# Cross attention on one Trainium2 core: a unit's softmax shift goes from TensorE to VectorE, and GpSimd pre-adds halves of exponentials

## The chip, the cores and the metric

One core of one Trainium2 chip runs the whole kernel; seven cores are idle. The metric is the device time of one execution in microseconds (us), from the chip's own clock. TensorE is PE in the profile, VectorE is DVE, ScalarE is ACT, GpSimd is POOL, SyncE is SP.

## The reference

The model is a small "audio tower": token selection, a retention layer, a top-1 mixture of experts, a cross attention, and a top-2 mixture of experts. The change is in the cross attention:

```
q = (text @ Wq.T + bq)          # 8 batches x 512 rows, 2 heads of 64
k = (video @ Wk.T + bk)         # 128 videos x 64 frames
v = (video @ Wv.T + bv)
logits = einsum('avhd,bthd->abhvt', k, q) / sqrt(64)
weights = softmax(logits, axis=3)        # over the 64 frames of one video
attn = einsum('avhd,abhvt->abhtd', v, weights).mean(over the 128 videos)
out = attn @ Wo.T + bo
```

Every one of the 4096 rows is scored against all 8192 frames in both heads, with a softmax of its own for each of the 128 videos: a maximum over 64 frames, a shift by it, an exponential, a sum over 64, a division.

## The kernel before, in words

The attention stage runs through **8 batches** of queries (`B`), in each through 16 chunks of 512 keys (`NKC`), and takes each chunk for the 512 rows of the batch in two **steps** of 256 rows. That is 32 steps to a batch (a "run" in the code) and 256 in all. A step works on four **units** (`UNITS`): unit j is one head (j % 2) and one tile of 128 rows (j // 2), its data 128 rows x 512 keys, that is 8 videos of 64 frames. Units 0 and 1 are pair 0, units 2 and 3 are pair 1. The logits of unit j live in bank j of `psL`, its weights in one of eight slots of `weights` (two parities of four).

What a unit goes through: two matmuls give the logits (L1754, L1755; queries split into a high and a low part); VectorE takes the negated maxima of a pair in one reduction of 128x1024 (L1840); the logits are shifted by them; ScalarE takes the exponential; VectorE sums the exponentials of a pair (L1856) and inverts the sums of all four units (L1862); GpSimd multiplies each unit's weights by them (L1945); TensorE transposes the weights, four blocks a unit (L1774); ScalarE copies the result out (L1908); TensorE multiplies by the values (L1788, "mix"), three steps after the logits.

Who does the shift is set by the table `SHIFTED_BY`: ScalarE for unit 0 (as the bias of eight small exponentials, L1901), TensorE for units 1 and 3 (one more matmul of the identity by the maxima into `psL`, L1764, then one exponential out of `psL`, L1893), VectorE for unit 2 (a tensor-tensor add out of `psL` into `weights`, L1850, then an exponential in place, L1896).

The order on each engine is written out by hand in its `step`. VectorE's step n before is: maximum of pair 0, `total(n - 1, ..., 1)`, `invert(n - 1)`, maximum of pair 1, the shift of unit 2, `total(n, ..., 0)`. TensorE's is: logits of pair 0, the shift of unit 3 of step n-1, transposes of pair 0 of step n-2, the mix of step n-3, the shift of unit 1, logits of pair 1, transposes of pair 1 of step n-2. GpSimd's is the four multiplications of step n-1, as soon as `invert(n - 1)` has run.

`steps_of` writes the first 8 steps of a run out flat (`FIRST`), where every semaphore count is a constant, and puts the other 24 in a hardware loop of 6 turns of 4 steps, where counts are computed in registers. In flat steps 1 and 3 the queries of the next batch are projected (L1746 on TensorE, L1886 on ScalarE, `low`, L1834, on VectorE).

An instruction that reads what its own engine has just written waits on a semaphore for it: the shift of unit 2 waits on `maxima_ready`, which the maximum just ahead of it raises, and then on `turned_ready`, since its slot of `weights` must have been transposed two steps before:

```
def subtract(n, parity, pair, reused):
    ...
        dve.wait_ge(maxima_ready, 2 * n + (pair + 1))
        if reused:
            dve.wait_ge(turned_ready, 4 * n + (j + 1 - 8))
        dve.tensor_tensor(...)
```

Of the kernel before, what the change touches and what calls it, by code (L numbers as in the profile page):

```python
# [20 lines left out]
ALU = mybir.AluOpType  # L21
# [1534 lines left out]
def cross_attention(nc, a, K):  # L1556
# [16 lines left out]
    with ExitStack() as ctx:  # L1573
# [10 lines left out]

        UNITS = 4
        STEPS, FIRST, LAG = 2 * NKC, 8, 3
        SHIFTED_BY = ("ScalarE", "TensorE", "VectorE", "TensorE")
        shifted_on = {who: [j for j in range(UNITS) if SHIFTED_BY[j] == who] for who in set(SHIFTED_BY)}
        keys_in = [sem(f"keys_in{s}") for s in range(2)]
        values_in = [sem(f"values_in{s}") for s in range(2)]  # L1590
# [58 lines left out]
        with ExitStack() as inner:  # L1649
# [15 lines left out]
            logits_ready, maxima_ready, exped = sem("logits_ready"), sem("maxima_ready"), sem("exped")  # L1665
            shifted, subtracted = sem("shifted"), sem("subtracted")
            summed, scales_ready, normalised = sem("summed"), sem("scales_ready"), sem("normalised")
            turned_ready, turned_copied = sem("turned_ready"), sem("turned_copied")
            chunks_mixed, run_copied = sem("chunks_mixed"), sem("run_copied")

# [36 lines left out]
            def exists(n):  # L1707

                return not isinstance(n, int) or 0 <= n < B * STEPS
# [4 lines left out]
            with nc.Block() as block:  # L1714
# [114 lines left out]
                @block.vector  # L1829
                def _(dve):  # L1830
                    def low(p, h, count):

                        dve.wait_ge(q_highs, count)
                        dve.scalar_tensor_tensor(q_low[p][h][:], psQ[:], K.bq2[:, h:h + 1], q_high[p][h][:].bitcast(F32),  # L1834
                                                 ALU.add, ALU.subtract).then_inc(q_lows, 1)

                    def maximum(n, pair):
                        dve.wait_ge(logits_ready, 4 * n + (2 * pair + 2))
                        both = slice(2 * pair, 2 * pair + 2)
                        dve.tensor_reduce(maxima[:, both, :].rearrange("p j v -> p (j v)"),  # L1840
                                          psL[:, both, :].rearrange("p j (v f) -> p (j v) f", f=FR), X, ALU.max, negate=True).then_inc(maxima_ready, 1)

                    def subtract(n, parity, pair, reused):
                        for j in (2 * pair, 2 * pair + 1):
                            if SHIFTED_BY[j] == "VectorE":
# [4 lines that stand above are left out]
                                dve.tensor_tensor(videos(weights[:, 4 * parity + j, :]), videos(psL[:, j, :]),  # L1850
                                                  maxima[:, j, :, None].bitcast(F32).to_broadcast([P, VC, FR]), ALU.add).then_inc(subtracted, 1)

                    def total(n, parity, pair):
                        both = slice(4 * parity + 2 * pair, 4 * parity + 2 * pair + 2)
                        dve.wait_ge(exped, 4 * n + (2 * pair + 6))
                        dve.tensor_reduce(sums[:, both, :].rearrange("p j v -> p (j v)"),  # L1856
                                          weights[:, both, :].rearrange("p j (v f) -> p (j v) f", f=FR), X, ALU.add).then_inc(summed, 1)

                    def invert(n, parity):
                        chunk = slice(4 * parity, 4 * parity + 4)  # L1860
                        dve.wait_ge(summed, 2 * n + 2)
                        dve.reciprocal(scales[:, chunk, :], sums[:, chunk, :]).then_inc(scales_ready, 1)  # L1862

                    def step(i, p, s, k, q4):
                        n, parity = index(i, p, s), k % 2
                        if exists(n):
                            maximum(n, 0)
                        if exists(n - 1):
                            total(n - 1, 1 - parity, 1)
                            invert(n - 1, 1 - parity)  # L1870
                        if exists(n):
                            maximum(n, 1)
                            subtract(n, parity, 1, exists(n - 2))
                            total(n, parity, 0)
                            if isinstance(s, int) and s in (1, 3):
                                low(1 - p, s // 2, (i * 2 + p) * 2 + (s // 2 + 3))

                    low(0, 0, 1)
                    low(0, 1, 2)
                    steps_of(dve, step)  # L1880
# [56 lines left out]

                @block.gpsimd
                def _(pool):
                    def normalise(n, parity, pair):  # L1940
                        for j in (2 * pair, 2 * pair + 1):
                            s = 4 * parity + j
# [4 lines left out]
                    def step(i, p, s, k, q4):  # L1947
                        n = index(i, p, s)
                        if exists(n - 1):
                            normalise(n - 1, 1 - k % 2, 0)  # L1950
                            normalise(n - 1, 1 - k % 2, 1)

                    steps_of(pool, step)
# [69 lines left out]
```

## Time and profile before

| | us |
|---|---|
| Time, median of 3 runs (2453.16 to 2456.1) | 2454.87 |
| Time of the profiled execution | 2457.68 |
| Span of the profiled execution | 2455.9 |
| Attention stage in it, about | 560 to 2140 |
| One step of the loop | 6.107 |
| One run of 32 steps | 197.14 |

The attention stage is two thirds of the time. Its steps repeat to within a hundredth of a microsecond, so that whatever a change does to one loop step it does 192 times (8 runs of 24), and to a flat step 64 times. In a timeline each row has the start of an instruction and its duration; two rows of one engine can overlap a little, so the cost of an instruction in a row of others is the distance from its start to the next start (called its pitch here), and not its duration.

### The profile page before, as it was taken

What the parts mean: (1) busy time and instruction counts of PE and PEld (TensorE: products, weight loads), DVE (VectorE), ACT (ScalarE), POOL (GpSimd) and SP (SyncE); (2) the same over time, 40 slices, a digit from 0 to 9 for tenths busy, and PEclk for the clock granted to TensorE, in tenths of its full rate; (3) what the DMA queues carried; (4) which work ended last, traced back from release to release, by engine and by line L of the source; (5) the groups of instructions that cost most, each with busy time, mean ns of one, the idle gap of its engine ahead of it and who ended that gap; (6) DMA issues with size and microseconds to landing.
All of it is one profiled execution on the core that took longest, in us unless ns stands there. A gap on an engine that the chain in (4) does not pass through costs nothing. (4 is left out here: it accounts for less than half of the span.)

```text
span 2455.9 us, 49808 instructions
## 1 busy us (share of the span) xinstructions
PE 2150.6 (88%) x14597; PEld 1692.2 (69%) x14597; DVE 1985.9 (81%) x3132; ACT 1689.1 (69%) x4826; POOL 1446.6 (59%) x1416
## 2 busy tenths in 40 slices
PE   4566876838999999999999999999999999967883
PEld 3345766825777777777777777777777777757883
DVE  6977764147999999999999999999999999866664
ACT  1154212516888888888888888888888888803662
POOL 2643433754666666666666666666666666623773
PEclk9675666968999999999999999999999999967997
DMA  7421023622222222222222222222222222143655
GB/s 242 142 69 44 28 60 94 168 60 61 65 64 65 65 64 64 65 64 64 65 64 64 65 64 64 65 64 64 65 65 64 64 65 64 43 96 101 156 154 154
DMA packets 157683, 197.68 MB, mean 80 GB/s; under 512 B 33200, under 2 KB 99888, under 8 KB 155504
## 3 DMA queue, kind: packets, MB, share of 16 engines
q1 hardware_dynamic: 139280, 174.80, 26.5%
q0 software_dynamic: 8064, 16.60, 2.5%
q10 hardware_dynamic: 10208, 4.66, 0.7%
q8 instruction: 67, 1.10, 0.2%
q14 instruction: 64, 0.52, 0.1%
HBM read 77.58 MB, written 17.74 MB: 39 GB/s over the span
## 5 line engine op out<-in xcount | busy, mean ns | idle before, releaser
L1945 POOL TENSOR_TENSOR attend_weights<-attend_weights,attend_scales 128x512 f32<-128x512 f32 x1024 | 1036.3, 1043 | 560.6 <-DVE attend_scales L1862 560.6
L1840 DVE TENSOR_REDUCE attend_maxima<-attend_psL 128x16 fp32r<-128x1024 f32 x512 | 624.5, 1220 | 89.5 <-PE attend_psL L1755 89.5
L1856 DVE TENSOR_REDUCE attend_sums<-attend_weights 128x16 f32<-128x1024 f32 x512 | 619.0, 1209 | 0.1
L1908 ACT ACTIVATE attend_turned<-attend_psT 128x512 f32<-128x512 f32 x1024 | 554.4, 596 | 9.0 <-PE attend_psT L1774 5.9
L1774 PE MATMUL attend_psT<-consts,attend_weights 128*128 128x128 f32 x4096 | 530.8, 272 | 0.8 <-POOL attend_weights L1945 0.8
L1774 PEld LDWEIGHTS attend_psT<-consts,attend_weights 128*128 128x128 f32 x4096 | 477.5, 140 | 66.1 <-POOL attend_weights L1945 1.3
L1788 PE MATMUL attend_psA<-attend_turned,attend_value_ring 128*64 128x256 f32 x4096 | 498.5, 385 | 0.8 <-ACT attend_turned L1908 0.8
L1901 ACT ACTIVATE attend_weights<-attend_psL,attend_maxima 128x64 f32<-128x64 f32 x2048 | 446.6, 329 | 53.1 <-DVE attend_maxima L1840 53.1
L1754 PE MATMUL attend_psL<-attend_key_ring,attend_q_high 128*128 128x512 f32 x1024 | 430.6, 420 | 1.6 <-ACT attend_q_high L1886 1.6
L1755 PE MATMUL attend_psL<-attend_key_ring,attend_q_low 128*128 128x512 f32 x1024 | 404.1, 395 | 0.0
L1788 PEld LDWEIGHTS attend_psA<-attend_turned,attend_value_ring 128*64 128x64 f32 x4096 | 271.5, 136 | 154.4 <-issue 43.7
L1893 ACT ACTIVATE attend_weights<-attend_psL 128x512 f32<-128x512 f32 x512 | 313.8, 613 | 0.0
L1896 ACT ACTIVATE attend_weights<-attend_weights 128x512 f32<-128x512 f32 x256 | 162.1, 633 | 128.6 <-DVE attend_weights L1850 128.5
L1764 PE MATMUL attend_psL<-attend_maxima,cross_ident_r 128*128 128x512 f32 x512 | 221.1, 432 | 6.1 <-DVE attend_maxima L1840 6.0
L1755 PEld LDWEIGHTS attend_psL<-attend_key_ring,attend_q_low 128*128 128x128 f32 x1024 | 194.6, 190 | 33.6 <-issue 3.8
L1754 PEld LDWEIGHTS attend_psL<-attend_key_ring,attend_q_high 128*128 128x128 f32 x1024 | 194.2, 190 | 30.3 <-issue 4.0
L1850 DVE TENSOR_TENSOR attend_weights<-attend_psL,attend_maxima 128x512 f32<-128x512 f32 x256 | 177.1, 692 | 25.8
L1764 PEld LDWEIGHTS attend_psL<-attend_maxima,cross_ident_r 128*128 128x128 f32 x512 | 95.9, 187 | 116.5 <-DVE attend_maxima L1840 99.6
L1448 ACT ACTIVATE moe2mix_hidT<-moe2mix_psH,moe_b 128x128 f32<-128x128 f32 x284 | 81.0, 368 | 57.6 <-PE moe2mix_psH L1401 57.4
L1363 POOL DMA_INDIRECT moe2mix_rows<-normed,moe_source x71 | 68.7, 968 | 79.0 <-POOLq L1134 50.9
L1862 DVE RECIPROCAL attend_scales<-attend_sums 128x32 f32<-128x32 f32 x256 | 90.4, 353 | 8.9
L1368 POOL DMA_INDIRECT result<-moe2mix_result,moe_target x71 | 70.8, 998 | 24.9 <-issue 16.8
(316 smaller groups left out, 2368.8 us busy)
## 6 DMA issues: line engine op xcount, KB each, us to landing
attend_key_ring<-keys SPq DMA_DIRECT2D x512, 128.0 KB, 2.2
attend_value_ring<-values SPq DMA_DIRECT2D x128, 256.0 KB, 2.5
moe2mix_w_tile<-in_L_ffn_w_dram SPq DMA_DIRECT2D x71, 256.0 KB
select_xbuf<-in_x_dram SPq DMA_DIRECT2D x16, 1024.0 KB, 5.4
moe1mix_w_tile<-in_L_ffn_W_dram SPq DMA_DIRECT2D x39, 256.0 KB, 3.1
select_emb<-L_attn_video_embeds_dram ACTq DMA_DIRECT2D x16, 256.0 KB, 4.3
values_gates<-project_vg SPq DMA_DIRECT2D x8, 512.0 KB, 2.6
retain_vg<-values_gates SPq DMA_DIRECT2D x8, 512.0 KB
```

Of the source, the lines that this page charges most:

```text
L1754: pe.matmul(psL[:, j, :], q_high[p][h][:, tile], key_ring[:, k // 2, h, :], start=True, stop=False, skip_group_check=True)
L1755: pe.matmul(psL[:, j, :], q_low[p][h][:, tile], key_ring[:, k // 2, h, :], start=False, stop=(SHIFTED_BY[j] != "TensorE"), skip_group_chec ...
L1764: pe.matmul(videos(psL[:, j, :]), ident_r[:], maxima[:, j, :, None].to_broadcast([P, VC, FR]), start=False, stop=True, skip_group_check=Tr ...
L1774: mm = pe.matmul(psT[:, j % 2, k * P:(k + 1) * P], weights[:, 4 * parity + j, k * P:(k + 1) * P], ident, is_transpose=True, start=(k == 0) ...
L1788: mm = pe.matmul(psA[head_rows(h), r * 2 * P:(r + 1) * 2 * P], value_ring[:, slot, h, t, :], turned[:, parity, t, h].rearrange("p t l -> p ...
L1840: dve.tensor_reduce(maxima[:, both, :].rearrange("p j v -> p (j v)"), psL[:, both, :].rearrange("p j (v f) -> p (j v) f", f=FR), X, ALU.ma ...
L1850: dve.tensor_tensor(videos(weights[:, 4 * parity + j, :]), videos(psL[:, j, :]), maxima[:, j, :, None].bitcast(F32).to_broadcast([P, VC, F ...
L1856: dve.tensor_reduce(sums[:, both, :].rearrange("p j v -> p (j v)"), weights[:, both, :].rearrange("p j (v f) -> p (j v) f", f=FR), X, ALU. ...
L1893: act.activation(into, psL[:, j, :], ACT.Exp).then_inc(exped, 1)
L1901: ins = act.activation(into[:, video], psL[:, j, video], ACT.Exp, bias=maxima[:, j, v:v + 1].bitcast(F32))
L1908: act.activation(turned[:, parity, :, h, t, :], psT[:, j % 2, :].rearrange("p (k q) -> p k q", k=SUB), ACT.Copy).then_inc(turned_copied, 1)
L1945: pool.tensor_tensor(w, w, scales[:, s, :, None].to_broadcast([P, VC, FR]), ALU.mult).then_inc(normalised, 1)
```

## The change

The second entry of `SHIFTED_BY` becomes VectorE, so that VectorE shifts units 1 and 2 and TensorE unit 3 alone. GpSimd gets a new instruction a step (`halve`): it adds the first 32 of every 64 exponentials of units 0 and 1 to the other 32, into a tile `halves` of 128x512, between its multiplications of units 0, 1 and of units 2, 3 of the step before. VectorE's sum of pair 0 then reads `halves` (512 elements) and not `weights` (1024), and stands one step later in the order: `total(n - 1, ..., 0)` beside `total(n - 1, ..., 1)`. The shift of unit 1 stands right behind the maximum of pair 0.

```diff
-        SHIFTED_BY = ("ScalarE", "TensorE", "VectorE", "TensorE")
+        SHIFTED_BY = ("ScalarE", "VectorE", "VectorE", "TensorE")
...
+            halves = sba("halves", [P, 2 * VC, FR // 2])
+            halved = sem("halved")
...
                     def total(n, parity, pair):
                         both = slice(4 * parity + 2 * pair, 4 * parity + 2 * pair + 2)
-                        dve.wait_ge(exped, 4 * n + (2 * pair + 6))
-                        dve.tensor_reduce(sums[:, both, :].rearrange("p j v -> p (j v)"),
-                                          weights[:, both, :].rearrange("p j (v f) -> p (j v) f", f=FR), X, ALU.add).then_inc(summed, 1)
+                        own = sums[:, both, :].rearrange("p j v -> p (j v)")
+                        if pair == 0:
+                            dve.wait_ge(halved, n + 1)
+                            dve.tensor_reduce(own, halves[:], X, ALU.add).then_inc(summed, 1)
+                        else:
+                            dve.wait_ge(exped, 4 * n + (2 * pair + 6))
+                            dve.tensor_reduce(own, weights[:, both, :].rearrange("p j (v f) -> p (j v) f", f=FR), X, ALU.add).then_inc(summed, 1)
...
                         if exists(n):
                             maximum(n, 0)
+                            subtract(n, parity, 0, exists(n - 2))
                         if exists(n - 1):
+                            total(n - 1, 1 - parity, 0)
                             total(n - 1, 1 - parity, 1)
                             invert(n - 1, 1 - parity)
                         if exists(n):
                             maximum(n, 1)
                             subtract(n, parity, 1, exists(n - 2))
-                            total(n, parity, 0)
...
+                    def halve(n, parity):
+
+                        pool.wait_ge(exped, 4 * n + 6)
+                        both = weights[:, 4 * parity:4 * parity + 2, :].rearrange("p j (v f) -> p (j v) f", f=FR)
+                        pool.tensor_tensor(halves[:], both[:, :, 0:FR // 2], both[:, :, FR // 2:FR], ALU.add).then_inc(halved, 1)
+
...
                             normalise(n - 1, 1 - k % 2, 0)
+                        if exists(n):
+                            halve(n, k % 2)
+                        if exists(n - 1):
                             normalise(n - 1, 1 - k % 2, 1)
```

VectorE's instructions of one loop step before. REGISTER_ALU and ISA rows are the sequencer's, which compute the count of a wait; L1849 stands between the wait on `maxima_ready` and the shift.

```order
L1840 TENSOR_REDUCE attend_maxima<-attend_psL 128x16
L1855 REGISTER_ALU
L1856 TENSOR_REDUCE attend_sums<-attend_weights 128x16
L1862 RECIPROCAL attend_scales<-attend_sums 128x32
L1838 REGISTER_ALU
L1840 TENSOR_REDUCE attend_maxima<-attend_psL 128x16
L1846 ISA
L1849 REGISTER_ALU
L1850 TENSOR_TENSOR attend_weights<-attend_psL,attend_maxima 128x512
L1855 REGISTER_ALU
L1856 TENSOR_REDUCE attend_sums<-attend_weights 128x16
L1838 ISA
```

And of one loop step of the change:

```order
L1842 TENSOR_REDUCE attend_maxima<-attend_psL 128x16
...
L1851 REGISTER_ALU
L1852 TENSOR_TENSOR attend_weights<-attend_psL,attend_maxima 128x512
L1860 TENSOR_REDUCE attend_sums<-attend_halves 128x16
L1862 REGISTER_ALU
L1863 TENSOR_REDUCE attend_sums<-attend_weights 128x16
L1868 RECIPROCAL attend_scales<-attend_sums 128x32
L1840 REGISTER_ALU
L1842 TENSOR_REDUCE attend_maxima<-attend_psL 128x16
L1848 REGISTER_ALU
L1851 REGISTER_ALU
L1852 TENSOR_TENSOR attend_weights<-attend_psL,attend_maxima 128x512
```

There is a second TENSOR_TENSOR behind the first maximum, with a register instruction of its own between the two; the last instruction of a step is a TENSOR_TENSOR where it was a sum.

TensorE in the middle of a loop step before, from the mix to the transposes of pair 1:

```order
L1788 MATMUL attend_psA<-attend_turned,attend_value_ring 64x256 x8
L1762 ISA
L1764 MATMUL attend_psL<-attend_maxima,cross_ident_r 128x512
L1753 REGISTER_ALU
L1754 MATMUL attend_psL<-attend_key_ring,attend_q_high 128x512
L1755 MATMUL attend_psL<-attend_key_ring,attend_q_low 128x512
```

And of the change:

```order
L1790 MATMUL attend_psA<-attend_turned,attend_value_ring 64x256 x8
L1755 REGISTER_ALU
L1756 MATMUL attend_psL<-attend_key_ring,attend_q_high 128x512
L1757 MATMUL attend_psL<-attend_key_ring,attend_q_low 128x512
L1755 REGISTER_ALU
```

The shift matmul behind the mix is gone, and with it TensorE's wait for the maxima of pair 0.

## Rows read from the trace of the kernel before

**Rows 1.** The page, part 1: busy time, share, instructions.
```profile
PE 2150.6 (88%) x14597; PEld 1692.2 (69%) x14597; DVE 1985.9 (81%) x3132; ACT 1689.1 (69%) x4826; POOL 1446.6 (59%) x1416
```
**Rows 2.** The page, part 5: busy us, mean ns, idle before and its releaser.
```profile
L1945 POOL TENSOR_TENSOR attend_weights<-attend_weights,attend_scales 128x512 f32<-128x512 f32 x1024 | 1036.3, 1043 | 560.6 <-DVE attend_scales L1862 560.6
L1840 DVE TENSOR_REDUCE attend_maxima<-attend_psL 128x16 fp32r<-128x1024 f32 x512 | 624.5, 1220 | 89.5 <-PE attend_psL L1755 89.5
...
L1764 PE MATMUL attend_psL<-attend_maxima,cross_ident_r 128*128 128x512 f32 x512 | 221.1, 432 | 6.1 <-DVE attend_maxima L1840 6.0
```
**Rows 3.** Timeline of VectorE, one loop step: start us, duration us.
```profile
1209.17 0.69 DVE L1850 TENSOR_TENSOR attend_weights<-attend_psL,attend_maxima 128x512 f32<-128x512 f32 x1
1209.78 1.21 DVE L1856 TENSOR_REDUCE attend_sums<-attend_weights 128x16 f32<-128x1024 f32 x1
1210.90 1.21 DVE L1840 TENSOR_REDUCE attend_maxima<-attend_psL 128x16 fp32r<-128x1024 f32 x1
1212.04 1.21 DVE L1856 TENSOR_REDUCE attend_sums<-attend_weights 128x16 f32<-128x1024 f32 x1
1213.28 0.35 DVE L1862 RECIPROCAL attend_scales<-attend_sums 128x32 f32<-128x32 f32 x1
1213.93 1.23 DVE L1840 TENSOR_REDUCE attend_maxima<-attend_psL 128x16 fp32r<-128x1024 f32 x1 [0.30 <-PE attend_psL L1755]
1215.28 0.69 DVE L1850 TENSOR_TENSOR attend_weights<-attend_psL,attend_maxima 128x512 f32<-128x512 f32 x1
```
**Rows 4.** Timeline of TensorE in that step: two shifts, transposes, mix.
```profile
1209.42 0.38 PE L1764 MATMUL attend_psL<-attend_maxima,cross_ident_r 128*128 128x512 f32 x1
1209.64 1.03 PE L1774 MATMUL attend_psT<-consts,attend_weights 128*128 128x128 f32 x8
1210.60 1.95 PE L1788 MATMUL attend_psA<-attend_turned,attend_value_ring 128*64 128x256 f32 x16
1212.48 0.48 PE L1764 MATMUL attend_psL<-attend_maxima,cross_ident_r 128*128 128x512 f32 x1
1212.80 0.40 PE L1754 MATMUL attend_psL<-attend_key_ring,attend_q_high 128*128 128x512 f32 x1
```
**Rows 5.** Timeline of ScalarE's exponentials of units 0 and 1, and of GpSimd.
```profile
1205.96 1.75 ACT L1901 ACTIVATE attend_weights<-attend_psL,attend_maxima 128x64 f32<-128x64 f32 x8 [0.17 <-DVE attend_maxima L1840]
1207.54 0.65 ACT L1893 ACTIVATE attend_weights<-attend_psL 128x512 f32<-128x512 f32 x1
...
1213.71 4.05 POOL L1945 TENSOR_TENSOR attend_weights<-attend_weights,attend_scales 128x512 f32<-128x512 f32 x4 [2.14 <-DVE attend_scales L1862]
```
**Rows 6.** Timeline of VectorE: inversions at one place of two runs, and a loop's end.
```profile
985.32 0.35 DVE L1862 RECIPROCAL attend_scales<-attend_sums 128x32 f32<-128x32 f32 x1
...
1182.46 0.35 DVE L1862 RECIPROCAL attend_scales<-attend_sums 128x32 f32<-128x32 f32 x1
...
1353.73 0.35 DVE L1862 RECIPROCAL attend_scales<-attend_sums 128x32 f32<-128x32 f32 x1
```
**Rows 7.** Timeline of VectorE in a flat step with `low` (L1834).
```profile
1176.43 1.23 DVE L1840 TENSOR_REDUCE attend_maxima<-attend_psL 128x16 fp32r<-128x1024 f32 x1 [0.39 <-PE attend_psL L1755]
1177.69 0.69 DVE L1850 TENSOR_TENSOR attend_weights<-attend_psL,attend_maxima 128x512 f32<-128x512 f32 x1
...
1179.42 0.74 DVE L1834 SCALAR_TENSOR_TENSOR attend_q_low<-attend_psQ,bq,attend_q_high 128x512 fp32r<-128x512 f32 x1
1180.08 1.21 DVE L1840 TENSOR_REDUCE attend_maxima<-attend_psL 128x16 fp32r<-128x1024 f32 x1
```
**Rows 8.** Groups by line and shape, other stages: reductions of VectorE, tensor-tensors of GpSimd.
```profile
L366 DVE TENSOR_REDUCE select_scores<-select_prod 128x16 f32<-128x2048 f32 x16 | 36.5, 2281 | 0.3
L618 DVE TENSOR_REDUCE retention_square<-project_squares 128x32 f32<-128x1024 f32 x8 | 9.8, 1220 | 0.3
...
L796 POOL TENSOR_TENSOR retain_swap<-retention_qk,retention_turn_s 128x512 f32<-128x512 f32 x8 | 14.1, 1767 | 38.4 <-POOLq L535 26.8 <-DVE retain_turn L900 11.5
L1624 POOL TENSOR_TENSOR hidden<-hidden,crossnorm_back 128x512 f32<-128x512 f32 x8 | 10.0, 1257 | 11.2 <-DMA crossnorm_back<-result 11.2
```

## The prediction

> **What bounds the kernel now.** Start with the page's busy times [rows 1]: TensorE 88%, VectorE 81%. The share says little about the attention stage, so go to the pitch of one step there. From one inversion in the loop to another 23 steps later it is (1353.73 - 1213.28) / 23 = 6.107 us [rows 3, 6]. Then ask in the timeline which engine has room in these 6.107 us.
>
> VectorE's step [rows 3], start to start: shift of unit 2 to sum of pair 0 0.61, sum to maximum 1.12 to 1.13, maximum to sum 1.13 to 1.14, sum to inversion 1.24, inversion to maximum 0.65, maximum to shift 1.35. That is 6.11, of which 0.30 is a wait for TensorE's logits ahead of the second maximum, and over the whole stage that wait is 89.5 us [rows 2]. It leaves VectorE 5.81 us of its own.
>
> TensorE has hardly a gap: only 6.1 us of waits stand before 512 shift matmuls [rows 2], and its pieces follow each other without a hole, shift to transposes 0.22, transposes to mix 0.96, mix to the next shift 1.88, that shift to the logits 0.32 [rows 4]. TensorE bounds the step, and VectorE is 0.30 us behind it. ScalarE and GpSimd wait for VectorE in every step (GpSimd 2.14 us [rows 5]).
>
> **The change, part by part.**
>
> TensorE loses one shift matmul a step: 0.22 us by the pitch of the first one, 0.32 by that of the second, the very one that goes [rows 4]. The extra 0.10 of the second may come with the turn from the 64-wide mix to a full-width matmul, and then the logits would inherit it. I take 0.22, with 0.32 as the other end: TensorE needs 5.89 us (5.79) after the change. If nothing else moved, 256 steps would give 56 us.
>
> VectorE's new loop step. The shift of unit 1 adds the pitch of a shift, 0.61. It stands right behind the maximum that it waits for, and this changes that maximum's pitch. A maximum followed by something independent costs 1.13 to 1.14 (1210.90 to 1212.04), a maximum followed by its own shift 1.35 (1213.93 to 1215.28) in the loop [rows 3] and 1.26 in a flat step (1176.43 to 1177.69) [rows 7]. The 0.12 are the wait for the end of the reduction in place of overlapping it; the other 0.09, there only in the loop, go with the register instruction that stands between the wait on the maxima and the shift. Both now apply to both maxima.
>
> The sum of pair 0 reads 512 elements instead of 1024. VectorE's reduction of 2048 takes 2281 ns [rows 8] and one of 1024 takes 1210 [rows 3], so 1024 elements cost 1.07 us and 512 cost 0.535. Groups of 32 rather than 64 cost nothing: 1024 in groups of 32 took 1220 [rows 8]. So this pitch goes from 1.13 to 0.59.
>
> The sum in the order of the new step: shift 2 to maximum 0.61 + maximum with own wait 1.35 + shift 1 0.61 + half sum 0.59 + full sum 1.24 + inversion 0.35 (its duration, now that no wait follows it) + maximum with own wait 1.35 = **6.10 us**. The VectorE work that the change adds eats the 0.30 us of room to the last hundredth: VectorE becomes the bound, at the same 6.10 at which TensorE bounds now. TensorE's saving turns into waiting. The 192 loop steps give 192 x 0.007 = 1.3 us.
>
> The flat steps are another matter. There VectorE pays 1.26 for each maximum with its shift: 6.10 - 0.18 = 5.92. A run takes 1182.46 - 985.32 = 197.14 us [rows 6]; less 24 x 6.107 this is 50.57 for its eight flat steps, 1.71 more than eight plain ones (the projections). After: on TensorE 8 x 5.89 + 1.71 = 48.83; on VectorE 8 x 5.92 and two `low` of 0.66 (1179.42 to 1180.08 [rows 7]), 48.68. The larger counts, 48.8: 1.8 us less a run, 14 in eight runs.
>
> GpSimd's new addition, 128x512 from two halves, has no equal in the trace. The nearest are the multiplication by the scales, 1043 [rows 2], an addition of two whole tiles, 1257, and at the dear end 1767 for one beside heavy VectorE work [rows 8]. I take 1.04 to 1.26, as its reads are like the middle one. GpSimd then works 4.05 + 1.26 = 5.3 of 6.1 us. Is `halves` there in time? Put the maximum of pair 0 at 0. The inversion runs from 3.79 to 4.14. GpSimd follows 0.08 behind it (1213.28 + 0.35 to 1213.71 [rows 3, 5]), ends units 0 and 1 at 6.26 and the halves at 7.5. VectorE wants them one step on at 6.10 + 1.96 = 8.06. There is 0.5 us of room, and even at 1767 ns it would just do. The exponentials of pair 0 that the addition reads are ready long before: ScalarE's eight small ones and the next take 2.23 us behind the maximum (1205.96 to 1207.54 + 0.65 [rows 5]). The multiplications of units 2 and 3 end 1.04 to 1.26 later than now, at 9.6, that is 3.5 in the next step; TensorE comes to transpose them at 3.6 and later.
>
> The other new wait is unit 1's on its slot of `weights`. TensorE transposes that slot when GpSimd has multiplied it, 6.26 - 6.10 = 0.16 in the next step, and is through some 0.6 later; the shift wants it at 1.35. From there, at about 0.8, TensorE has its mix to do, 1.88, and then what is left of its step of before, 6.11 - 0.22 - 0.96 - 1.88 - 0.32 = 2.73, about a third of it each for the logits of pair 1, transposes and the logits of pair 0. The logits of pair 1 are there at 3.6 and those of pair 0 at 5.4, against the maxima at 4.14 and 6.10. So nothing but VectorE's own sequence sets the step. Nor does GpSimd disturb VectorE as it is now: the shift of unit 2 takes its 0.69 beside GpSimd's multiplications or without them [rows 3, 5].
>
> Sum: -14 in the flat steps, -1.3 in the loop, against the profiled 2457.68: 2442. The median of the runs is 2.8 us lower, hence 2439; I say **2440**.
>
> A rule that would give another time: the Trainium skill (VectorE: DVE Perf Modes, The DRAIN you can't avoid) says that every VectorE instruction waits for the pipe to empty anyway, so that a semaphore between chained ones costs nothing. By it the step on VectorE would be 5.66 us and not 6.10. The rows speak against it here, with 1.35 against 1.13 for the same reduction, and the rows decide the sum; it is the first of the rivals.
>
> **The rivals.**
>
> *Own waits cost nothing.* If both maxima had the pitch 1.13, VectorE's step would be 6.10 - 0.44 = 5.66, TensorE's 5.79 to 5.89 would bound, and 256 x 0.22 to 0.32 would give 2373 to 2399. Against it stand 1.35 and 1.26. Half of it can be: that the register instruction's 0.09 is hidden at one maximum, since other instructions stand around it. That is 192 x 0.09 = 17, 2422. Together 0.12.
>
> *The loop's end shows on VectorE (slower).* Every fourth step ends with a register instruction and a branch. Now a sum of 1.12 pitch stands over them and the timeline shows nothing of them; after the change the last instruction is a shift with 0.61. If the branch needs all of the 1.12, each of the 48 loop turns pays 0.51 more, 25 us: 2465. It passes "no change" (2455) at 0.31 a turn, and 2460 at 0.41. Nothing in the trace prices it from below, except that no engine shows a longer step at a turn's end. 0.12 for the slower part, 0.12 for a part of it that ends within 0.2%. The Trainium skill (Advanced Engine Details and Errata) gives 108 ns for compare-and-branch, which would be hidden; no row here shows it.
>
> *VectorE waits for the halves.* GpSimd would have to be over 0.5 us later than worked out. Each 0.1 beyond costs 26 us over the 256 steps, 2466. Its rows are steady, 4.05 for four; 0.04, slower.
>
> *The change does nothing*: the flat steps too are held, by `low` waiting for the projected queries now that one sum less stands ahead of it. Then only 2 us go, 2453. 0.08.
>
> The main forecast, VectorE as the new bound with loop steps of 6.07 to 6.12: 2432 to 2446, 0.52.
>
> **How the numbers follow.** About 0.2% (4.9 us) is what a measurement of this kernel can tell from no change. Faster: main case and the cheaper waits, 0.64 and some for a gain of the second pitch (0.32) in the flat steps, 0.65. Same: 0.12 + 0.08, 0.20. Slower: 0.15. The range goes from 2422 (the register instruction hidden once) to 2458 (most of a loop's end exposed).
>
> **What the profile would show.** TensorE's share falls, and it shows waits, for GpSimd's `weights` ahead of the transposes or for the maxima; VectorE has no wait ahead of either maximum in the loop; loop steps between 6.07 and 6.12 and flat ones near 5.9; the halves' reduction near 670 ns; GpSimd's addition 1.04 to 1.26 us; L1764 x256. The prediction falls if a loop step is off 6.10 by more than 0.1 (19 us), if the maximum of pair 0 has a pitch other than 1.35, or if turn ends show a gap.

## The result and the profile after

The changed kernel takes 2426.32 us (median of 4 runs, 2424.38 to 2427.76) beside 2454.01 for the kernel before: ratio 0.9879, with a 95% interval of 0.9863 to 0.9895. By the medians it is 27.7 us faster, where the forecast of 2440 against 2454.87 was 14.9: nearly twice the gain. VectorE became the bound, as forecast, but its loop step came out shorter than worked out.

The page of the changed kernel, parts 1 and 5 (busy us, mean ns, idle before it and its releaser):

```profile
PE 2112.0 (87%) x14341; PEld 1631.3 (67%) x14341; DVE 2004.9 (83%) x3388; ACT 1674.1 (69%) x4826; POOL 1762.8 (73%) x1672
...
L1842 DVE TENSOR_REDUCE attend_maxima<-attend_psL 128x16 fp32r<-128x1024 f32 x512 | 618.5, 1208 | 4.7 <-PE attend_psL L1757 2.7
...
L1951 POOL TENSOR_TENSOR attend_halves<-attend_weights 128x512 f32<-128x512 f32 x256 | 326.2, 1274 | 16.6 <-ACT attend_weights L1903 16.6
...
L1860 DVE TENSOR_REDUCE attend_sums<-attend_halves 128x16 f32<-128x512 f32 x256 | 173.1, 676 | 1.4 <-POOL attend_halves L1951 1.4
...
L1766 PE MATMUL attend_psL<-attend_maxima,cross_ident_r 128*128 128x512 f32 x256 | 98.0, 383 | 1.8 <-DVE attend_maxima L1842 1.8
```

Against [rows 1, 2]: the 512 shift matmuls are 256. VectorE's wait for logits ahead of its maxima fell from 89.5 us to 2.7 of 4.7 idle, so VectorE has used up its room. How close TensorE still is can be seen in a timeline of the two engines where the second maximum of a step begins:

```profile
1304.73 0.40 PE L1757 MATMUL attend_psL<-attend_key_ring,attend_q_low 128*128 128x512 f32 x1
...
1305.17 1.22 DVE L1842 TENSOR_REDUCE attend_maxima<-attend_psL 128x16 fp32r<-128x1024 f32 x1
```

The last logits matmul ends at 1305.13 (a modelled end), the maximum begins at 1305.17.

On the page, GpSimd's addition takes 1274 ns, near the 1257 of the whole-tile addition of [rows 8]. The half sum takes 676 ns against 1210, as worked out.

VectorE's timeline in the changed kernel (start us, duration us): flat step 1 of a run with `low` (L1836), inversions at one place of two runs, and one loop step, which answers to [rows 3, 6, 7]:

```profile
966.93 0.35 DVE L1868 RECIPROCAL attend_scales<-attend_sums 128x32 f32<-128x32 f32 x1
967.39 1.23 DVE L1842 TENSOR_REDUCE attend_maxima<-attend_psL 128x16 fp32r<-128x1024 f32 x1
...
969.85 0.75 DVE L1836 SCALAR_TENSOR_TENSOR attend_q_low<-attend_psQ,bq,attend_q_high 128x512 fp32r<-128x512 f32 x1 [0.51 <-ACT attend_q_high L1893]
...
974.21 0.35 DVE L1868 RECIPROCAL attend_scales<-attend_sums 128x32 f32<-128x32 f32 x1
...
991.88 0.35 DVE L1868 RECIPROCAL attend_scales<-attend_sums 128x32 f32<-128x32 f32 x1
...
1185.19 0.35 DVE L1868 RECIPROCAL attend_scales<-attend_sums 128x32 f32<-128x32 f32 x1
...
1205.34 1.22 DVE L1842 TENSOR_REDUCE attend_maxima<-attend_psL 128x16 fp32r<-128x1024 f32 x1
1206.68 0.69 DVE L1852 TENSOR_TENSOR attend_weights<-attend_psL,attend_maxima 128x512 f32<-128x512 f32 x1
1207.29 0.68 DVE L1860 TENSOR_REDUCE attend_sums<-attend_halves 128x16 f32<-128x512 f32 x1
1207.88 1.21 DVE L1863 TENSOR_REDUCE attend_sums<-attend_weights 128x16 f32<-128x1024 f32 x1
1209.13 0.35 DVE L1868 RECIPROCAL attend_scales<-attend_sums 128x32 f32<-128x32 f32 x1
1209.39 1.22 DVE L1842 TENSOR_REDUCE attend_maxima<-attend_psL 128x16 fp32r<-128x1024 f32 x1
1210.74 0.69 DVE L1852 TENSOR_TENSOR attend_weights<-attend_psL,attend_maxima 128x512 f32<-128x512 f32 x1
1211.35 1.21 DVE L1842 TENSOR_REDUCE attend_maxima<-attend_psL 128x16 fp32r<-128x1024 f32 x1
```

The loop step, from 1205.34, start to start: maximum with its shift behind it 1.34, shift 0.61, half sum 0.59, full sum 1.25, inversion **0.26**, maximum 1.35, shift 0.61, together 6.01. The next takes 5.97. Averaged over 22 loop steps of the same trace (from 1010 us on) the seven terms are 1.33, 0.61, 0.59, 1.25, 0.27, 1.32 and 0.61, together 5.98. Between the inversions at 991.88 and 1185.19 lie 193.31 us, against 197.14 [rows 6].

The loop steps average 5.985 us, 0.122 less than before, which makes 24 x 0.122 = 2.9 us a run; the eight flat steps give the other 0.9. Eight runs give some 31 us in the profiled execution, about 23 of them in the loop, where 1.3 were forecast, and about 7 in the flat steps, where 14 were.

### The profile page after: what moved, and what is told of

Read it like the earlier page. It is cut to its first block and busy times, and to the rows that moved or that the text cites. A ratio compares the mean times of both kernels' runs of the same rounds, so it can differ in the third digit from the quotient of the medians.

```text
span 2422.3 us, 50062 instructions
## 1 busy us (share of the span) xinstructions
PE 2112.0 (87%) x14341; PEld 1631.3 (67%) x14341; DVE 2004.9 (83%) x3388; ACT 1674.1 (69%) x4826; POOL 1762.8 (73%) x1672
## 5 line engine op out<-in xcount | busy, mean ns | idle before, releaser
L1958 POOL TENSOR_TENSOR attend_weights<-attend_weights,attend_scales 128x512 f32<-128x512 f32 x1024 | 1047.1, 1044 | 198.4 <-DVE attend_scales L1868 198.4
L1776 PE MATMUL attend_psT<-consts,attend_weights 128*128 128x128 f32 x4096 | 553.9, 275 | 4.6 <-POOL attend_weights L1958 2.0
L1756 PE MATMUL attend_psL<-attend_key_ring,attend_q_high 128*128 128x512 f32 x1024 | 457.7, 447 | 3.9 <-ACT attend_weights L1908 2.3
L1903 ACT ACTIVATE attend_weights<-attend_weights 128x512 f32<-128x512 f32 x512 | 342.3, 669 | 135.6 <-DVE attend_weights L1852 135.6
L1852 DVE TENSOR_TENSOR attend_weights<-attend_psL,attend_maxima 128x512 f32<-128x512 f32 x512 | 354.2, 692 | 52.7 <-DVE attend_maxima L1842 2.0
L1951 POOL TENSOR_TENSOR attend_halves<-attend_weights 128x512 f32<-128x512 f32 x256 | 326.2, 1274 | 16.6 <-ACT attend_weights L1903 16.6
L1863 DVE TENSOR_REDUCE attend_sums<-attend_weights 128x16 f32<-128x1024 f32 x256 | 309.7, 1210 | 0.0
L1860 DVE TENSOR_REDUCE attend_sums<-attend_halves 128x16 f32<-128x512 f32 x256 | 173.1, 676 | 1.4 <-POOL attend_halves L1951 1.4
L1900 ACT ACTIVATE attend_weights<-attend_psL 128x512 f32<-128x512 f32 x256 | 148.3, 579 | 0.1
L1766 PE MATMUL attend_psL<-attend_maxima,cross_ident_r 128*128 128x512 f32 x256 | 98.0, 383 | 1.8 <-DVE attend_maxima L1842 1.8
```

The source lines that it names most:

```text
L1756: pe.matmul(psL[:, j, :], q_high[p][h][:, tile], key_ring[:, k // 2, h, :], start=True, stop=False, skip_group_check=True)
L1776: mm = pe.matmul(psT[:, j % 2, k * P:(k + 1) * P], weights[:, 4 * parity + j, k * P:(k + 1) * P], ident, is_transpose=True, start=(k == 0) ...
L1863: dve.tensor_reduce(own, weights[:, both, :].rearrange("p j (v f) -> p (j v) f", f=FR), X, ALU.add).then_inc(summed, 1)
L1903: act.activation(into, into, ACT.Exp).then_inc(exped, 1)
L1951: pool.tensor_tensor(halves[:], both[:, :, 0:FR // 2], both[:, :, FR // 2:FR], ALU.add).then_inc(halved, 1)
L1958: pool.tensor_tensor(w, w, scales[:, s, :, None].to_broadcast([P, VC, FR]), ALU.mult).then_inc(normalised, 1)
```

## The experiments

Eleven kernels ran in three sets, each beside the kernel before on the same chip. The diffs are against the changed kernel. The chips of the first two sets (experiments 1 to 6, without `order_inversion`) needed 2519 us for the kernel before, the others 2454 to 2456. A loop step bound by TensorE has the same 6.11 us there (experiment 2) as in the kernel before, so ratios and steps are compared, not times.

### 1. The table without GpSimd's addition (`table_only`)

```diff
-                        if pair == 0:
-                            dve.wait_ge(halved, n + 1)
-                            dve.tensor_reduce(own, halves[:], X, ALU.add).then_inc(summed, 1)
-                        else:
...
+                        dve.wait_ge(exped, 4 * n + (2 * pair + 6))
+                        dve.tensor_reduce(own, weights[:, both, :]..., X, ALU.add).then_inc(summed, 1)
...
-                        if exists(n):
-                            halve(n, k % 2)
```

> The change without GpSimd's addition: VectorE shifts units 1 and 2, and sums all 1024 exponentials of both pairs. Theory V (VectorE's own sequence sets the step of the changed kernel, 5.98 us): the full sum costs 0.53 us more than the half one, the step is 6.51, 256 x 0.53 = 136 us over the changed kernel, about 2563 us, and slower than before. Rival T (what was gained is TensorE's relief from the shift, and VectorE has room): no slower than the changed kernel by more than 20 us, 2426 to 2446.

Ratio 1.0331 (1.0315 to 1.0347), slower than before. VectorE in the loop, where it waits for nobody:

```profile
1195.94 0.35 DVE L1864 RECIPROCAL attend_scales<-attend_sums 128x32 f32<-128x32 f32 x1
1196.21 1.16 DVE L1842 TENSOR_REDUCE attend_maxima<-attend_psL 128x16 fp32r<-128x1024 f32 x1
1197.49 0.69 DVE L1852 TENSOR_TENSOR attend_weights<-attend_psL,attend_maxima 128x512 f32<-128x512 f32 x1
1198.10 1.21 DVE L1842 TENSOR_REDUCE attend_maxima<-attend_psL 128x16 fp32r<-128x1024 f32 x1
1199.44 0.69 DVE L1852 TENSOR_TENSOR attend_weights<-attend_psL,attend_maxima 128x512 f32<-128x512 f32 x1
...
1202.42 0.35 DVE L1864 RECIPROCAL attend_scales<-attend_sums 128x32 f32<-128x32 f32 x1
```

The step is 6.48 us, 0.03 under the 6.51 of the expectation. Against the changed kernel the ratio rose by 0.045, some 111 us, and not by 136: the plain flat steps went only to 6.30, and the two with `low` stayed at 7.27. Rival T, that TensorE's relief by itself is the gain, is out: with TensorE relieved in the same way the kernel loses 3.3%. VectorE's own sequence sets this step. Its rows also give the sizes that the prediction had wrong. From the inversion to the shift behind the next maximum it is 1197.49 - 1195.94 = 1.55 us, where the forecast had 0.35 + 1.35 = 1.70. Less the half sum's saving this VectorE-only step is 6.48 - 0.535 = 5.94.

### 2. GpSimd's halves alone (`halves_only`)

```diff
-        SHIFTED_BY = ("ScalarE", "VectorE", "VectorE", "TensorE")
+        SHIFTED_BY = ("ScalarE", "TensorE", "VectorE", "TensorE")
```

> GpSimd's halves and the later sum alone; unit 1 is shifted by TensorE as before. Theory V for the changed kernel says that before TensorE bounds at 6.107 and VectorE only gets more room: no change against before, 2450 to 2458. Rival S (the shorter sum is by itself the gain, since VectorE was in the loop that sets the step before): 2426 or lower.

Ratio 1.000 (0.9991 to 1.0009). VectorE now waits 0.92 for the logits, where it waited 0.30 [rows 3]:

```profile
1223.02 0.35 DVE L1868 RECIPROCAL attend_scales<-attend_sums 128x32 f32<-128x32 f32 x1
1224.29 1.23 DVE L1842 TENSOR_REDUCE attend_maxima<-attend_psL 128x16 fp32r<-128x1024 f32 x1 [0.92 <-PE attend_psL L1757]
...
1229.13 0.35 DVE L1868 RECIPROCAL attend_scales<-attend_sums 128x32 f32<-128x32 f32 x1
```

The step is 6.11 as before, bound by TensorE. Neither half of the change gains anything alone: the table costs 3.3%, the halves give nothing, and together they give 1.2%.

### 3. The other order of the two waits (`wait_order`, `table_wait_order`)

```diff
-                                dve.wait_ge(maxima_ready, 2 * n + (pair + 1))
                                 if reused:
                                     dve.wait_ge(turned_ready, 4 * n + (j + 1 - 8))
+                                dve.wait_ge(maxima_ready, 2 * n + (pair + 1))
```

> The changed kernel with the two waits of a shift in the other order: first on the slot of the weights, then on the maxima, so that the register instruction runs while the maximum still runs. If the 0.09 us by which a maximum and its shift are longer in the loop than in a flat step come from that register instruction, VectorE's loop step falls by 0.18 to 5.80, TensorE's need of 5.79 to 5.89 may take over, and 192 x 0.09 to 0.18 = 17 to 35 us go: 2391 to 2409. If they come from elsewhere, 2426.

> The table and order of the change without GpSimd's addition, and with the waits of a shift in the other order. Here VectorE alone bounds (6.48 us a loop step, 6.30 a flat one), so that the price of the register instruction shows whole. If it is that: 0.09 less at each of two maxima in the 192 loop steps, step 6.30 in the loop too, about 34 us less than the same kernel with the old order of waits: ratio to before 1.0331 - 0.0137 = 1.019. Rival: the loop itself (fetch, branch) makes the steps longer, the ratio stays at 1.033.

On the changed kernel: ratio 0.9834 (0.9821 to 0.9848). That is 0.0045 or 11 us less than the changed kernel, short of the 17 to 35 expected, though clear of no change. Its loop steps take 5.90, which alone would give 16 us. On the table-only kernel, where VectorE alone bounds: 1.0227 (1.021 to 1.0243), its loop step now 6.30 to the hundredth (from 1253.60 on; the two inversions ahead of it are of flat steps):

```profile
1240.79 0.35 DVE L1864 RECIPROCAL attend_scales<-attend_sums 128x32 f32<-128x32 f32 x1
...
1247.23 0.35 DVE L1864 RECIPROCAL attend_scales<-attend_sums 128x32 f32<-128x32 f32 x1
...
1253.60 0.35 DVE L1864 RECIPROCAL attend_scales<-attend_sums 128x32 f32<-128x32 f32 x1
1253.87 1.16 DVE L1842 TENSOR_REDUCE attend_maxima<-attend_psL 128x16 fp32r<-128x1024 f32 x1
1255.06 0.69 DVE L1852 TENSOR_TENSOR attend_weights<-attend_psL,attend_maxima 128x512 f32<-128x512 f32 x1
1255.67 1.22 DVE L1842 TENSOR_REDUCE attend_maxima<-attend_psL 128x16 fp32r<-128x1024 f32 x1
1256.92 0.69 DVE L1852 TENSOR_TENSOR attend_weights<-attend_psL,attend_maxima 128x512 f32<-128x512 f32 x1
...
1259.90 0.35 DVE L1864 RECIPROCAL attend_scales<-attend_sums 128x32 f32<-128x32 f32 x1
```

A maximum with its shift costs 1.19 and 1.25 here, against 1.28 and 1.34 in the rows of experiment 1. So the order of the waits is worth 0.09 at each of the two maxima in the loop, and the rival, that the loop itself makes its steps longer, is out. That the 0.09 is the register instruction which stood between the two waits, as the prediction had it, is the reading that fits best: flat steps with the old order, where no such instruction stands, have the same 1.19 and 1.25 (`table_only`, from 1215.56 us on). It is not the whole account of the order, because in the flat steps the same edit costs something. They went from 6.30 to 6.44 (1240.79 to 1247.23), since each maximum with its shift takes 0.07 more there, though both waits are on constants. Why the order of two such waits matters is open. It is also why the total fell by some 26 us and not by the 34 expected.

### 4. What bounds once VectorE is relieved

Four TensorE rows of the changed kernel with the other order of waits: the shift of unit 3, the first two logits matmuls of pair 1, which stand right behind the mix, and the next shift of unit 3:

```profile
1230.14 0.38 PE L1766 MATMUL attend_psL<-attend_maxima,cross_ident_r 128*128 128x512 f32 x1
...
1233.20 0.50 PE L1756 MATMUL attend_psL<-attend_key_ring,attend_q_high 128*128 128x512 f32 x1
1233.54 0.40 PE L1757 MATMUL attend_psL<-attend_key_ring,attend_q_low 128*128 128x512 f32 x1
...
1236.04 0.38 PE L1766 MATMUL attend_psL<-attend_maxima,cross_ident_r 128*128 128x512 f32 x1
```

From one shift to the next it is 5.90 us, and the second maximum now follows the logits: the inversion ahead of it has a pitch of 0.34 here on average, against 0.27 in the changed kernel. The first logits matmul behind the mix has the pitch 0.34 (1233.20 to 1233.54), as the shift matmul in its place had 0.32 [rows 4]: the 0.10 came with the place and not with the shift, and the saving of TensorE was 0.22. Its need is the forecast 5.89. To test that VectorE had room again, the inversion was written twice, with the old and with the new order of waits:

```diff
                         dve.reciprocal(scales[:, chunk, :], sums[:, chunk, :]).then_inc(scales_ready, 1)
+                        dve.reciprocal(spare_scales[:, chunk, :], sums[:, chunk, :])
```

> The changed kernel with every inversion written a second time into a tile that nobody reads. Theory V (VectorE's sequence sets the step; an inversion followed by something independent costs 0.27 us, not its duration of 0.35): the step goes from 5.985 to 5.95 + 0.27 = 6.22, 256 x 0.24 = 60 us more than the changed kernel, ratio to before 0.988 + 0.024 = 1.012. If its pitch is the 0.35 of the prediction: 80 us more, 1.020. Rival (TensorE or GpSimd sets the step and VectorE has room): under 10 us more, 0.988 to 0.992.

> The other order of waits everywhere and a second inversion. Theory V+T: VectorE alone needs 5.95 - 0.18 + 0.215 = 5.985 a loop step, TensorE 5.90, so of the 0.215 only 0.085 shows in the loop: step 5.98 to 6.00, about 20 us over the kernel with the order of waits alone, ratio 0.991 to 0.993. Rival (VectorE still sets the 5.90 by itself): all 0.215 show, 6.11, 256 x 0.215 = 55 us, ratio 1.005.

With the old order: ratio 1.002 (1.0011 to 1.003), step 6.15, where 1.012 and 6.22 were expected. VectorE's rows:

```profile
1254.28 0.35 DVE L1869 RECIPROCAL attend_scales<-attend_sums 128x32 f32<-128x32 f32 x1
1254.54 0.30 DVE L1870 RECIPROCAL attend_spare_scales<-attend_sums 128x32 f32<-128x32 f32 x1
1254.76 1.16 DVE L1843 TENSOR_REDUCE attend_maxima<-attend_psL 128x16 fp32r<-128x1024 f32 x1
...
1260.43 0.35 DVE L1869 RECIPROCAL attend_scales<-attend_sums 128x32 f32<-128x32 f32 x1
```

The first inversion has the pitch 0.26, the second 0.22 (I had put in 0.27 for it). 5.94 + 0.215 = 6.155 is the step, so this VectorE-only kernel and the table-only one agree on 5.94 for the changed kernel. The rival by which VectorE has room is out, as is the 0.35.

With the new order: ratio 0.9909 (0.9894 to 0.9924), loop step 5.975, a few thousandths under what was expected. Only 0.075 of the 0.215 showed. So with the new order VectorE by itself needs 5.76 (5.975 less 0.215), and it was TensorE that held the step at 5.90:

```profile
1253.72 0.35 DVE L1869 RECIPROCAL attend_scales<-attend_sums 128x32 f32<-128x32 f32 x1
...
1259.70 0.35 DVE L1869 RECIPROCAL attend_scales<-attend_sums 128x32 f32<-128x32 f32 x1
```

### 5. The half sum between the maximum and its shift (`half_between`)

```diff
                             maximum(n, 0)
-                            subtract(n, parity, 0, exists(n - 2))
                         if exists(n - 1):
                             total(n - 1, 1 - parity, 0)
+                        if exists(n):
+                            subtract(n, parity, 0, exists(n - 2))
+                        if exists(n - 1):
                             total(n - 1, 1 - parity, 1)
```

> The changed kernel with the half sum moved between the maximum of pair 0 and the shift of unit 1, so that neither waits for the instruction just ahead. Theory V: maximum 1.13 instead of 1.34, the rest as it is, VectorE needs 5.77; then TensorE's need of 5.79 to 5.89 shows, and the step is that: 256 x 0.09 to 0.19 = 23 to 49 us less, 2377 to 2403. Rival T' (TensorE or the chain through GpSimd already sets 5.98): 2426.

Ratio 1.0051 (1.0038 to 1.0065): slower than before, outside both theories. VectorE and GpSimd together show why:

```profile
1248.92 0.35 DVE L1868 RECIPROCAL attend_scales<-attend_sums 128x32 f32<-128x32 f32 x1
...
1249.35 2.05 POOL L1960 TENSOR_TENSOR attend_weights<-attend_weights,attend_scales 128x512 f32<-128x512 f32 x2 [0.91 <-DVE attend_scales L1868]
...
1251.35 1.28 POOL L1953 TENSOR_TENSOR attend_halves<-attend_weights 128x512 f32<-128x512 f32 x1
...
1252.67 0.69 DVE L1860 TENSOR_REDUCE attend_sums<-attend_halves 128x16 f32<-128x512 f32 x1 [0.37 <-POOL attend_halves L1953]
...
1253.27 0.68 DVE L1852 TENSOR_TENSOR attend_weights<-attend_psL,attend_maxima 128x512 f32<-128x512 f32 x1
1253.87 1.21 DVE L1863 TENSOR_REDUCE attend_sums<-attend_weights 128x16 f32<-128x1024 f32 x1
...
1255.11 0.35 DVE L1868 RECIPROCAL attend_scales<-attend_sums 128x32 f32<-128x32 f32 x1
```

VectorE waits 0.37 for the halves. The step is a ring through GpSimd: inversion, 0.43 until GpSimd starts, 3.3 us there (two multiplications and the addition), half sum 0.60, shift 0.60, full sum 1.24, inversion again, 6.19 us. The prediction had worked out 0.5 us of room for the halves in the changed kernel and made its loss a rival. That held there. This edit asks for them some 0.8 us sooner (the shift's 0.61 and the 0.2 by which the maximum was to be shorter), and I had not taken the room off in its expectation. So this run says nothing of the two theories that it was made for.

### 6. The low part of the queries one step later (`low_later`, `order_and_low`)

The rows of the changed kernel in flat step 1, from 966.93 to 974.21 in the timeline of the result, show what the prediction had not seen. The step takes 7.28 us, not 5.92 + 0.66 = 6.58. `low` waits 0.51 for ScalarE's copy of the queries that TensorE has just projected, and the inversion ahead has a pitch of 0.46 where it can have 0.27. Before, the sum of pair 0 stood between the shift and `low`, and covered it.

```diff
-                            if isinstance(s, int) and s in (1, 3):
-                                low(1 - p, s // 2, (i * 2 + p) * 2 + (s // 2 + 3))
...
                             total(n - 1, 1 - parity, 0)
+                            if exists(n) and isinstance(s, int) and s in (2, 4):
+                                low(1 - p, s // 2 - 1, (i * 2 + p) * 2 + (s // 2 + 2))
```

> The changed kernel with the low part of the next queries (L1836) one step later on VectorE, behind the half sum. The trace of the changed kernel shows 0.51 us of wait ahead of it in flat steps 1 and 3 and 0.19 ahead of the next maxima, 7.28 us for such a step against the 6.58 of the prediction. Theory: these waits are what the flat steps gave less than forecast, 16 x 0.5 to 0.7 = 8 to 11 us less than the changed kernel, ratio 0.9835 to 0.9848. Rival: TensorE's projection holds the two steps anyway: 0.988.

> The changed kernel with both: the other order of waits and the later low part. Theory: TensorE bounds at 5.90 in the loop, and the flat steps lose their waits; the two gains add where they lie in different steps: 0.9834 - 0.003 to 0.004 = 0.979 to 0.981, the fastest version here. Rival: TensorE also holds the flat steps at 5.90, and the later low part gives nothing on top: 0.983.

Ratios 0.9899 (0.9884 to 0.9914) and, with the new order of waits as well, 0.9845 (0.9832 to 0.9858): nothing gained against 0.9879 and 0.9834. The wait has only moved, from `low` to the next maximum:

```profile
1374.95 0.35 DVE L1868 RECIPROCAL attend_scales<-attend_sums 128x32 f32<-128x32 f32 x1
...
1378.08 1.22 DVE L1842 TENSOR_REDUCE attend_maxima<-attend_psL 128x16 fp32r<-128x1024 f32 x1 [0.71 <-PE attend_psL L1757]
...
1380.54 0.74 DVE L1836 SCALAR_TENSOR_TENSOR attend_q_low<-attend_psQ,bq,attend_q_high 128x512 fp32r<-128x512 f32 x1
```

These are VectorE's rows; TensorE's beside them are the projection and the last logits matmul of pair 1:

```profile
1376.09 1.02 PE L1748 MATMUL attend_psQ<-cross_normT,wq 128*128 128x512 f32 x2
...
1377.65 0.39 PE L1757 MATMUL attend_psL<-attend_key_ring,attend_q_low 128*128 128x512 f32 x1
```

The maximum waits 0.71 us for logits that stand behind the projection in TensorE's queue: they end at 1378.04, and it begins at 1378.08. That much of the rival, that TensorE's projection holds the step, is borne out. TensorE does not set the two steps alone, though. From mix to mix it takes 6.76 us in the step with the projection and 6.49 in the next, where it needs 5.89. What holds it in that next step was not taken apart.

### 7. The other order of waits in the loop alone (`order_in_loop`), and the change again

```diff
-                                dve.wait_ge(maxima_ready, 2 * n + (pair + 1))
+                                def maximum_done():
+                                    dve.wait_ge(maxima_ready, 2 * n + (pair + 1))
+                                if isinstance(n, int):
+                                    maximum_done()
                                 if reused:
                                     dve.wait_ge(turned_ready, 4 * n + (j + 1 - 8))
+                                if not isinstance(n, int):
+                                    maximum_done()
```

> The changed kernel with the other order of waits in the loop alone; the flat steps keep the old one, since the flat steps of the table-only kernel went from 6.30 to 6.44 us with the new order. Theory: loop 5.90 by TensorE, flat steps as in the changed kernel: 192 x 0.085 = 16 us less than the changed kernel, ratio 0.981 to 0.983, the fastest here. Rival: TensorE holds the flat steps at its 5.89 as well, and it is the same as with the new order everywhere: 0.9834.

> The changed kernel itself, beside the others on the same chip: its ratio should be again 0.988 with steps of 5.985 in the loop.

The change came out at 0.9869 (0.9854 to 0.9884) here, the new order in the loop alone at **0.9801 (0.9788 to 0.9815)**, the fastest of all: 17 us under the change, and a little better than the 0.981 to 0.983 expected. Its loop steps average 5.89, TensorE's bound, and its flat steps keep the 5.77 and 7.28 of the changed kernel.

## Why the prediction was right or wrong, point by point

- **What bounds.** TensorE before and VectorE after: right. With the halves alone, more room on VectorE changed nothing. In the changed kernel VectorE hardly waits, and 0.215 us more of VectorE work lengthened the step by 0.17.
- **TensorE's need of 5.89 us**: right, measured as 5.89 to 5.90 where VectorE was relieved. The other end, 5.79, is out.
- **The half sum, the added shift, GpSimd's addition**: 0.59, 0.61 and 1.27 against 0.59, 0.61 and 1.04 to 1.26. Right, the last at the upper end.
- **Own waits of 1.35 in the loop at both maxima.** The place was right, and the cause fits every run with the two waits swapped in the loop. One size was wrong: behind an inversion that nothing holds up, the maximum with its shift costs 1.28 to 1.29 and not 1.35, when VectorE alone sets the pace. Both rows from which the 1.35 and the flat 1.26 were read ([rows 3], [rows 7]) stand right behind a wait for logits, and the maximum lasts 1.23 us in them; without the wait it lasts 1.16 (experiment 1). The Trainium skill (VectorE: DVE Perf Modes, The DRAIN you can't avoid) tells of eight copies in a row for which a semaphore after each cost nothing extra. These traces do not agree for this reduction: it costs 1.13 ahead of something independent [rows 3] and 1.25 ahead of its own shift with the waits at their best, in the rows of experiment 3.
- **"inversion 0.35 (its duration, now that no wait follows it)": this is the step that failed.** The pitch is 0.26 to 0.27. Every other term of that sum was a pitch, start to start; this one was a duration, taken because the trace before has a wait behind nearly every inversion. The idle time that a row shows is counted from the end of the inversion's duration, so VectorE's room before was nearer 0.38 us a step than the 0.30 that was read. All instructions of VectorE in [rows 3] overlap their successor by about 0.08 when they do not have to be finished first, and so does this one. With the 0.07 of the maximum it makes 0.15 us a step: 6.10 should have been 5.94 to 5.95. The step became 5.985, and the rest is again in that maximum, which with its shift costs 1.32 on average in the changed kernel and not 1.28. TensorE's logits arrive there only hundredths of a microsecond ahead of it, and its duration reads 1.18 to 1.22 and not 1.16. That the one causes the other is a reading, not a test. The difference from 6.10 is 0.115 x 192 = 22 us, 15 of them by the inversion. The flat steps took 7 back, so that the total was off by less. The loop step also broke the prediction's own condition, to be within 0.1 of 6.10.
- **Room of the logits of pair 1**, "at 3.6 against 4.14": too generous. They come at 4.01 against 4.05 (1305.13 and 1305.17 in the result's second view, the maximum of pair 0 being at 1301.12). Part of it is that the mix begins 1.06 us on average behind the transposes ahead of it, and not 0.96 as in [rows 4], which fits a wait for GpSimd's unit 1. More of it is that the four logits matmuls last 1.19 us to the end of the last, where the prediction put a third of 2.73, which is 0.91.
- **The flat steps, -14 us**: about -7. The plain ones took 5.76 to 6.02, on average somewhat under the forecast 5.89 to 5.92 (with the 0.08 and the 0.07 taken off, VectorE's sum is 5.77 there too). But two in each run took 7.15 to 7.29. The wait of `low` was named as a rival ("one sum less stands ahead of it"), at 0.08, and it happened in part. It was not put into the sum, and experiment 6 did not win it back.
- **The loop's end exposed**: it did not happen. No fourth step is longer than the others, with 0.61 of cover instead of 1.12.
- **GpSimd late**: not in the changed kernel; experiment 5 shows how near it was.

## What to carry to other kernels

When a sum decides between two engines that end within 2% of each other, take every term as a start-to-start distance in a stretch without waits; a duration in their midst was 0.08 us too long here, which is 15 us over the 192 loop steps, as much as the whole forecast gain. When an engine's instruction waits for the one just ahead of it and for something else, put the wait for the one just ahead last in a hardware loop, so that the counts can be worked out while that one still runs (0.09 us each here), and check the flat copies of the loop apart, because there the same order lost 0.07 us. Moving a reader earlier spends the room of its producer: look for the ring that closes through the third engine first.

## What the runs showed of the hardware that was not expected

In flat code, where both waits of an instruction are on constants, their order made 0.07 us of difference to VectorE (1.19 to 1.26 and 1.25 to 1.32 us for a maximum with its shift), with no instruction between them. In the loop the order made 0.09 the other way. The first is unexplained.

The kernel before took 2519 us beside experiments 1 to 6 and 2454 to 2456 beside the others, on other chips, while TensorE-bound attention steps were equal. The traces show where the difference lies. From its first logits matmul to its last mix the attention stage takes 1588 us in the kernel before and 1587 with the halves alone (`halves_only`, on a chip of 2519). Ahead of it 560 us go in the one and 584 in the other, and behind it 308 and 350. So it is all outside the attention stage, and what causes it there is open. The same reading gives the changed kernel 1555 us in one profiled execution and 1558 in the other.
